# Second convolution by four phases of the position on 32-by-32 array tiles, one read-back of its input, other PSUM banks at the end

## The chip, the cores and the metric

The kernel runs on one core of a Trainium2 chip. The metric is the device time of one execution in microseconds; the median of three runs before the change is 1615.36 us (1615.16 to 1615.81). The program is written by hand for five engines (TensorE, VectorE, ScalarE, GpSimd, and SyncE, which issues every DMA); each engine has its own list of instructions and waits on semaphores.

## The reference, cut to what matters

`x` is 64 sequences of 32 tokens of 512 numbers. The last lines of the reference are a residual chain: a conditional mix of channels and a state-space block with group norm and output projection are added to `x`, then a grouped one-dimensional convolution with a context term, then a feed-forward layer with a cluster mask:

```
x = x + attn(cond(x, cond_128, ...), ...)
x = x + cond2(x, cond_128, weight, c_weight, bias=fside)   # what the change is about
x = x + ffn(x, weight, bias, centroids, assignments)
```

The convolution treats the 32 tokens of a sequence as channels and the 512 numbers as positions: 32 channels in, 32 out, 4 groups of 8 channels, 9 taps, padding 4:

```
out = lax.conv_general_dilated(x, weight, (1,), [(4, 4)], ('NCH','OIH','NCH'), feature_group_count=4)
out = out + einsum('nd,od->no', c, c_weight)[:, :, None] + bias[None, :, None]
```

The feed-forward layer computes `x @ weight.T + bias` (512 by 512), a softmax over 64 clusters, and zeroes rows and columns by whether any softmax value passes 0.01. The kernel's FFN takes the convolution's result as its input, and its output is added to the running `x`.

## The kernel before, in words

A token tile is four sequences, 128 tokens, on 128 partitions; there are 16 of them, T = 0 to 15, held for the whole run in `acc[128, 16, 520]` with four zero columns at either side of the 512. The main part is a loop over 32 stages (`stage(n)`, L556 on TensorE), each a pair of a half of the batch and one of 8 groups; a stage projects ten 128-row blocks (`proj`, L421) with fp32r high and low parts, and between them runs the scan's small matmuls (`Y`, L497, `G_all`, L484), the output projection of the stage before (`O`, L531) and its statistics (`S`, L516). `add_out` (L1084) adds the result to `acc`. The last stage is called END (n = 31). The diff changes nothing in the loop but access patterns.

After the last stage comes the part that the change is about. SyncE writes each finished tile to DRAM (`store_x2`, L307) and reads it back as `G_of(T)` with tokens as channels (`load_G`, L312): the input of the convolution for one tile is read four times, each time shifted by one position, so that partition 32j + channel holds the sequence shifted by j. `load_G` has four DMAs of 260 KB each per tile, into two tensors (`wh`, `wl`) that held projection weights.

TensorE then computes the convolution in pairs of tiles. `conv2(T)` (L589) covers taps 0 to 3 and 4 to 7: for each of four sequences one matmul of 128 rows by 32 columns over 512 positions, twice, into the PSUM bank `PP[T % 2]`. `conv2_last_tap(T)` (L600) covers tap 8 for both tiles of the pair with 32-by-32 matmuls, each (sequence, tile) on another row strip of the array. All these are plain fp32 matmuls; in the trace one fp32 matmul is two MATMUL instructions.

Per tile, ScalarE copies the convolution's bank to SBUF with the context bias (`x3_biased`, L854), TensorE transposes it (`turn`, L610, four 128-column transposes, alternately into banks 6 and 3), ScalarE and VectorE split it into high and low parts (`x3_high`, L862; `x3_low`, L1153), and TensorE multiplies by the feed-forward weights in two column halves of 288 (`ffn(T, 1)`, `ffn(T, 0)`, L622). VectorE's `ffn_rows(T)` (L1167) handles maximum, softmax sums, mask and bias; `dense` (L1157) reads the FFN's banks.

TensorE's program after stage 31 (L669 to L700) is: `conv2(0)`, `conv2(1)`, `conv2_last_tap(0)`, then the rest of END (`O(END, 0)`, `Y`, `O(END, 1)`, `S`, `turn(0)`, `O(END, 2)`, `O(END, 3)`, `S`), then steps 2 to 17. A step s is: on even steps below 16 the convolution of tiles s and s + 1, then `turn(s - 1)`, `ffn(s - 2, 1)`, and for tiles below LATE = 10 also `ffn(s - 2, 0)`. The halves `ffn(T, 0)` of tiles 10 to 15 come after the last step. Then the column maximum is transposed (L694), the mask of rows is spread by matmuls (L697, L698), `choose` (L1200, VectorE) writes the results of tiles 4 to 15 to `acc`, `finish_apart` (L1391, GpSimd) those of tiles 0 to 3, and SyncE stores them in the order `order_out`. For tiles 10 to 15 GpSimd runs `late_base` (L1380) beforehand.

At the start SyncE loads `x`: tiles 0 to 3 by four DMAs (L285), tiles 4 to 15 by three DMAs of 1 MB (L292), and then projection blocks one by one into a ring of three (`load_w`, L294). GpSimd makes the low part of each block (`split_w_lo`, L1315) and two thirds of the mixing weights (`mixing_weights`, L1304).

Of the kernel before, what the change touches and what calls it, by code (L numbers as in the profile page):

```python
# [22 lines left out]
P_CW, P_CB, P_D, P_NW, P_B0, P_B1, P_DTB, P_AL, P_FS, P_END = 0, 192, 240, 272, 304, 305, 306, 307, 308, 309  # L23
# [7 lines left out]
FB = ((SEG[0], PP[2]), PY)  # L31
# [47 lines left out]
def before(n, i, back=2):  # L79
    return divmod(4 * n + i - back, 4)  # L80

# [5 lines left out]
def adaln_attn_ffn_kernel(nc, x, emb, gin, b2, wbank, biask, w_in, w_dt, w_out, prm, cst, cw4, ctxw,  # L87
                          w_ffn, b_ffn, asg, x2s, out):
    ctx = ExitStack()
    with ctx:  # L90
# [48 lines left out]
        cxb = sb("cxb", [128, NT])  # L139
# [27 lines left out]
        cxt = yq[:, 128:192].rearrange("p (t b) -> p t b", b=4)  # L167
# [10 lines left out]
        asi, asf, ohf = xs[0:64, 2, :].bitcast(I32), xs[0:64, 3, :], Lt[0:64, 0:512]  # L178
# [3 lines left out]

        def G_of(T):
            w = (wh, wl)[(T % 4) // 2][:, :, :].rearrange("p a b -> p (a b)").bitcast(F32)
            return w[:, 2080 * (T % 2):2080 * (T % 2) + 2080].rearrange("p (b c) -> p b c", b=4)
# [8 lines left out]
        def ffn_bank(T, c):  # L194
            if c == 0 and T >= LATE + 2:
                return (PP[0], PP[1], FB[0][1], FB[1][1])[T - LATE - 2]
            return FB[T % 2][c]

# [3 lines left out]
        def O_bank(n, i):  # L202
            return PP[2] if (n, i) == (END, 1) else PO[i]
# [13 lines left out]
        ld_x = [None] + [signal(f"ld_x{c}", step=16) for c in range(1, 4)]  # L217
# [4 lines left out]
        ld_G = [signal(f"ld_G{r}", [(T, j) for T in range(r, NT, 4) for j in range(4)], 16) for r in range(4)]  # L222
# [39 lines left out]
        conv_ok, x3_ok, x3t = signal("cv", range(NT)), signal("x3", range(NT)), signal("xt", range(NT))  # L262
# [13 lines left out]
        def sync_program(e):  # L276
# [7 lines left out]
            for T in range(4):  # L284
                e.dma_start(acc[:, T, 4:516], x[T]).then_inc(ld_x0[T].sem, 16)  # L285
# [26 lines left out]
            def load_G(T):  # L312
                sp.wait_ge(x2_out[T // 4], 4 * (T // 4) + 3)
                if T < 4:
                    sp.wait_ge(proj_ok, (END, 4 if T % 2 == 0 else 8))
                else:
                    sp.wait_ge(conv_ok, T - 4)
# [24 lines left out]
            for T in (0, 2, 1, 3):  # L342
                load_G(T)
# [3 lines left out]
            sp.wait_ge(T_ok, (END, 3))  # L347
            for j in range(4):
                sp.wait_ge(xsd_ok, (END, j))
# [3 lines left out]
            for T in range(4, NT):  # L353
                if T == 9:
                    for t in range(12, 16):
                        store_x2(t)
                load_G(T)
# [4 lines left out]
        def tensor_program(e):  # L362
# [7 lines left out]
            def mix_tile(T, n):  # L370
# [19 lines left out]
                for k in range(4):  # L390
                    mm = e.matmul(PS[:, bank, 128 * k:128 * k + 128], acc[:, T, 4 + 128 * k:132 + 128 * k], bd,  # L391
# [124 lines left out]
            def S(n, group):  # L516
                pe.wait_ge(ys2, (n, group[-1]))
                if group[0] == 0:
                    if n:
                        pe.wait_ge(var_ok, (n - 1, 3))  # L520
                    else:
                        pe.wait_ge(cx_ok, 0)
                elif group == (1, 2):
# [3 lines left out]
                for i in group:  # L527
                    mm = e.matmul(PS[:, PG, 256 + i:257 + i], yss[:, i, :], C[:, C_ONE:C_ONE + 1], start=True, stop=True)  # L528
                mm.then_inc(S_ok.sem, 1)

            def O(n, i):  # L531
# [8 lines left out]
                elif i == 1:  # L540
                    pe.wait_ge(evac_ok, (n, 7))
                else:
                    pe.wait_ge(y_ok, (n, 3))
                q = 0
# [6 lines left out]
            def context():  # L551
                pe.wait_ge(ld_cx)
                pe.wait_ge(G_masked, 0)
                e.matmul(PS[:, PG, 128:192], yq[:, 0:128], eT, start=True, stop=True).then_inc(cx_pe.sem, 1)
# [34 lines left out]
            def conv2(T):  # L589
                pe.wait_ge(ld_G[T % 4], (T, 3))  # L590
                if T >= 2:
                    pe.wait_ge(x3_ok, T - 2)
                else:
                    pe.wait_ge(evac_ok, (END, 8 + T))
                for q, off in enumerate((0, 4)):
                    for b in range(4):
                        e.matmul(PS[32 * b:32 * b + 32, PP[T % 2], :], w4[:, q, :], G_of(T)[:, b, off:off + 512],  # L597
                                 start=(q == 0), stop=False)

            def conv2_last_tap(T):  # L600
                for b in range(4):
                    for t in (T, T + 1):
                        r = (b + t) % 4
                        p = slice(32 * r, 32 * r + 32)
                        mm = e.matmul(PS[32 * b:32 * b + 32, PP[t % 2], :], w4[p, 2, :], G_of(t)[p, b, 8 - r:520 - r],
                                      start=False, stop=True)
                        if b == 3:
# [901 lines left out]
```

## Time and profile before

| | before |
|---|---|
| median of 3 runs | 1615.36 us |
| profiled execution, its own time | 1614.37 us |
| its span, first to last instruction | 1612.4 us |
| TensorE busy | 1587.4 us, 98% |
| VectorE busy | 1049.8 us, 65% |
| ScalarE busy | 845.7 us, 52% |
| GpSimd busy | 787.5 us, 49% |
| mean granted TensorE clock | 0.997 |
| DMA, data moved | 93.19 MB |

Times in the trace are counted from the span's start. The profiled execution took 2.0 us more than its span. Matmul durations in the trace overlap each other, since matmuls are pipelined; the time that a row of the chain of waits gives to a run of matmuls does not overlap with the next row, so the prediction takes its costs there.

### The profile page before, as it was taken

The numbers are of one execution on the slowest core, as the hardware profiler recorded it, in microseconds if no ns is written. First come the engines' busy times: TensorE is split into PE (matmuls) and PEld (weight loads), VectorE is DVE, ScalarE is ACT, GpSimd is POOL, SyncE is SP. The second block draws the span as 40 slices with busy tenths as digits, with TensorE's granted clock in tenths as the row PEclk, the third lists the DMA queues.
The fourth block names the chain that finished last, engine by engine and source line by source line (L and its number), as shares of the span: only waits on it lengthen the run. The fifth ranks groups of instructions, "written<-read, shape, count | busy, mean of one in ns | idle before, by whom it ended". The sixth has DMA issues, their size and how long they took to land.

```text
span 1612.4 us, 32430 instructions
## 1 busy us (share of the span) xinstructions
PE 1587.4 (98%) x13001; PEld 1275.0 (79%) x13001; DVE 1049.8 (65%) x1707; ACT 845.7 (52%) x1372; POOL 787.5 (49%) x747
## 2 busy tenths in 40 slices
PE   8999999999999999999999999999999999999998
PEld 6778888888888888877777888888888888888666
DVE  6876666565656667576776656565766656565545
ACT  4654546555555555555455555555555655554321
POOL 3564645546363644544345454536454554633306
PEclk9999999999999999999999999999999999999999
DMA  5111102011111102011012111112020111113892
GB/s 191 59 54 33 41 21 66 28 53 40 40 53 34 51 12 64 27 53 40 22 50 77 53 40 40 54 34 59 10 64 21 53 40 47 47 36 85 200 210 107
DMA packets 50293, 93.19 MB, mean 58 GB/s; under 512 B 5664, under 2 KB 6304, under 8 KB 50144
## 3 DMA queue, kind: packets, MB, share of 16 engines
q1 hardware_dynamic: 50144, 91.11, 19.6%
q8 instruction: 104, 1.70, 0.5%
q14 instruction: 45, 0.37, 0.1%
HBM read 82.64 MB, written 8.45 MB: 56 GB/s over the span
## 4 chain that ended last, share of the span: by engine, by line
PE 86%; ACT 6%; DVE 3%; issue 3%; POOL 2%; POOLq 0%; DVEq 0%; ACTq 0%
PE PS L438 49%; PE PS L547 20%; PE PS L513 4%; PE PS L481 3%; PE PS L639 2%; ACT L798 2%; PE PS L597 2%; ACT big L791 1%; PE PS L528 1%; ACT Lt L798 1%; DVE cb L1023 1%; PE PS L391 1%; PE PS L493 1%; ACT oh L717 1%; PE PS L388 1%
## 5 line engine op out<-in xcount | busy, mean ns | idle before, releaser
L438 PE MATMUL PS<-xh,wh 128*128 128x512 f32 x1280 | 520.0, 406 | 0.6 <-DVE xl L955 0.6
L438 PE MATMUL PS<-xh,wl 128*128 128x512 f32 x1280 | 500.3, 391 | 0.0
L438 PE MATMUL PS<-xl,wh 128*128 128x512 f32 x1280 | 500.2, 391 | 0.0
L1023 DVE SCALAR_TENSOR_TENSOR cb<-PS,P,cb 128x496 f32<-128x496 f32 (+2 forms) x576 | 412.4, 716 | 130.6 <-ACT cb L759 117.0
L1318 POOL TENSOR_TENSOR wl<-rw,wh 128x512 fp32r<-128x512 f32 x160 | 212.6, 1334 | 187.4 <-ACT wh L710 172.3
L1338 POOL TENSOR_TENSOR ysum<-yq 128x256 f32<-128x256 f32 x128 | 109.4, 855 | 361.7 <-ACT yq L806 361.7
L438 PEld LDWEIGHTS PS<-xh,wl 128*128 128x128 f32 x1280 | 240.5, 188 | 53.1
L438 PEld LDWEIGHTS PS<-xh,wh 128*128 128x128 f32 x1280 | 240.8, 188 | 51.4 <-issue 1.0
L438 PEld LDWEIGHTS PS<-xl,wh 128*128 128x128 f32 x1280 | 241.2, 188 | 44.6
L759 ACT ACTIVATE cb<-PS,P 128x512 f32<-128x512 f32 x192 | 148.5, 774 | 205.1 <-PE PS L438 205.1
L1053 DVE TENSOR_TENSOR big<-Lt,gmt 128x512 f32<-128x512 f32 x128 | 102.3, 841 | 153.4 <-ACT Lt L798 153.4
L547 PE MATMUL PS<-oh,yh 128*128 128x512 f32 x512 | 200.0, 391 | 0.3 <-issue 0.3
L547 PE MATMUL PS<-oh,yl 128*128 128x512 f32 x512 | 199.2, 389 | 0.0
L547 PE MATMUL PS<-ol,yh 128*128 128x512 f32 x512 | 199.2, 389 | 0.0
L806 ACT ACTIVATE yq<-y 128x512 f32<-128x512 f32 x128 | 81.0, 633 | 209.0 <-DVE y L1067 196.7
L766 ACT ACTIVATE big<-PS 128x512 f32<-128x512 f32 x128 | 76.2, 595 | 148.6 <-PE PS L438 148.2
L781 ACT ACTIVATE big<-cb 128x512 f32<-128x512 f32 x192 | 119.5, 623 | 63.4 <-DVE cb L1023 63.4
L1092 DVE SCALAR_TENSOR_TENSOR acc<-PS,rs,acc 128x512 f32<-128x512 f32 x128 | 93.1, 749 | 84.5 <-issue 46.9
L1355 POOL TENSOR_TENSOR rs<-vr,mh 128x1 f32<-128x1 f32 (+1 forms) x95 | 57.0, 600 | 164.4 <-DVE vr L1082 164.3
L1043 DVE TENSOR_TENSOR dtx<-PS,dtt 128x512 f32<-128x512 f32 x128 | 82.0, 682 | 59.9 <-PE PS L481 59.6
L547 PEld LDWEIGHTS PS<-oh,yh 128*128 128x128 f32 x512 | 96.1, 188 | 21.0 <-issue 0.8
L547 PEld LDWEIGHTS PS<-oh,yl 128*128 128x128 f32 x512 | 96.1, 188 | 20.0
(204 smaller groups left out, 2177.6 us busy)
## 6 DMA issues: line engine op xcount, KB each, us to landing
rw<-in_w_in SPq DMA_DIRECT2D x160, 256.0 KB, 2.7
ro<-in_w_out SPq DMA_DIRECT2D x64, 256.0 KB, 2.8
x2s<-acc SPq DMA_DIRECT2D x16, 260.0 KB, 5.4
out_x<-acc SPq DMA_DIRECT2D x16, 256.0 KB, 2.6
acc<-in_x SPq DMA_DIRECT2D x3, 1024.0 KB, 9.4
wh<-x2s SPq DMA_DIRECT2D x8, 260.0 KB, 5.0
wl<-x2s SPq DMA_DIRECT2D x8, 260.0 KB, 5.7
wh<-x2s SPq DMA_DIRECT2D x8, 259.5 KB, 5.6
```

The lines of the kernel that those rows point to most:

```text
L438: mm = e.matmul(PS[:, proj_bank(n, m), :], w[:, m, 128 * k:128 * k + 128], v[:, k, a:a + 512], start=(i == 0), stop=(i == 11))
L547: mm = e.matmul(PS[:, O_bank(n, i), :], v[:, r, 128 * j:128 * j + 128], w[:, j, :], start=(q == 0), stop=(q == 11))
L759: e.activation(cb[:, z % 2, :], PS[:, proj_bank(n, m), :], ACT.Identity, bias=P[:, P_CB + c:P_CB + c + 1], scale=P[:, P_CW + 4 * c + 3:P_C ...
L766: e.activation(gate[:, m - 6, :], PS[:, proj_bank(n, m), :], ACT.Silu).then_inc(evac_ok.sem, 1)
L781: e.activation(dst, cb[:, (6 * n + m) % 2, :], ACT.Silu).then_inc(silu_ok.sem, 1)
L806: e.activation(yq[:, :], y[:, i % 2, :], ACT.Square).then_inc(yq_ok.sem, 1)
L1023: e.scalar_tensor_tensor(out=cv[:, :, d:32], in0=pv[:, :, 0:32 - d], scalar=P[:, P_CW + 4 * c + 3 - d:P_CW + 4 * c + 4 - d], in1=cv[:, :, ...
L1043: e.tensor_tensor(dtx[:, r, :].rearrange("p (j v c) -> p j v c", j=4, v=2), PS[:, b0:b0 + 2, 256 * r:256 * r + 256].rearrange("p v (j c) - ...
L1053: e.tensor_tensor(Mb[:, i % 2], bc(Lt[:, 256 * i:256 * i + 256].rearrange("p (h o t) -> p h o t", h=8, o=1), 128, 8, 2, 32), bc(gmt[:, i, ...
L1092: e.scalar_tensor_tensor(out=acc[:, T, 4:516], in0=PS[:, O_bank(n, i), :], scalar=rs[:, i:i + 1], in1=acc[:, T, 4:516], op0=ALU.mult, op1= ...
L1318: e.tensor_tensor(wl[:, m, :], rw[:, q % RW, :], f(wh[:, m, :]), ALU.subtract).then_inc(w_lo.sem, 1)
L1338: e.tensor_tensor(ysum[:, :], yq[:, 0:256], yq[:, 256:512], ALU.add).then_inc(ys1.sem, 1)
```

## The change

The 512 positions of a token are stored phase by phase: position 4j + f stands at column 128f + j. Inputs, projection weights, output weights and FFN weights are permuted on the host, and the output is permuted back. In `acc` each phase has one zero column on either side (4 times 130 = 520). So a partition of the read-back tensor can hold one (channel, phase) pair, and a group of 8 channels with 4 phases fills 32 partitions. A convolution output of phase f' is then a sum over three shifts a of the phase columns: 3 matmuls of 32 by 32 over 128 columns for each channel group, sequence and tile.

`conv2(c)` now does four tiles, 4c to 4c + 3, in one go, with 4 x 3 x 4 x 4 = 192 matmuls on all 16 array tiles. Output channel group g goes to PSUM bank g, so the four banks 0 to 3 hold four token tiles. The input is read back once per tile (one DMA in pieces of 520 bytes instead of four DMAs). The loads and the final stores of `acc` are in pieces of 512 bytes.

```diff
-            def conv2(T):
-                pe.wait_ge(ld_G[T % 4], (T, 3))
-                if T >= 2:
-                    pe.wait_ge(x3_ok, T - 2)
-                else:
-                    pe.wait_ge(evac_ok, (END, 8 + T))
-                for q, off in enumerate((0, 4)):
-                    for b in range(4):
-                        e.matmul(PS[32 * b:32 * b + 32, PP[T % 2], :], w4[:, q, :], G_of(T)[:, b, off:off + 512],
-                                 start=(q == 0), stop=False)
-            def conv2_last_tap(T):
...
+            def conv2(c):
+                if c:
+                    pe.wait_ge(x3_ok, (4 * c - 1, 3))
+                else:
+                    pe.wait_ge(evac_ok, (END, 9))
...
+                pe.wait_ge(ld_G[c], 4 * c + 3)
+                for t in range(4):
+                    for a in range(3):
+                        for k in range(4):
+                            for b in range(4):
+                                g = (b + k) % 4
+                                p = slice(32 * g, 32 * g + 32)
+                                mm = e.matmul(PS[32 * b:32 * b + 32, g, 128 * t:128 * t + 128], w4[p, a, :],
+                                              G_of(4 * c + t)[p, b, a:a + 128], start=(a == 0), stop=(a == 2))
+                mm.then_inc(conv_ok.sem, 1)
```

The read-back, the loads and the stores on SyncE:

```diff
-                for j in range(4):
-                    src = bass.AP(x2s.tensor, T * 128 * XP + j, [[XP, 32], [32 * XP, 4], [1, 520 - j]])
-                    e.dma_start(G_of(T)[32 * j:32 * j + 32, :, 0:520 - j], src).then_inc(ld_G[T % 4].sem, 16)
+                src = bass.AP(x2s.tensor, T * 128 * XP, [[XP // 4, 128], [32 * XP, 4], [1, XP // 4]])
+                e.dma_start(G_of(T), src).then_inc(ld_G[T // 4].sem, 16)
...
-                e.dma_start(acc[:, T, 4:516], x[T]).then_inc(ld_x0[T].sem, 16)
+                e.dma_start(tokens(T), phases(x[T])).then_inc(ld_x0[T].sem, 16)
...
-            e.dma_start(yq[:, 0:128], ctxw).then_inc(ld_cx.sem, 16)
+            e.dma_start(Lt[:, 512:1024], ctxw).then_inc(ld_cx.sem, 16)
             for c in range(1, 4):
-                e.dma_start(acc[:, 4 * c:4 * c + 4, 4:516], x[4 * c:4 * c + 4].rearrange("t p d -> p t d")).then_inc(ld_x[c].sem, 16)
+                for T in range(4 * c, 4 * c + 4):
+                    e.dma_start(tokens(T), phases(x[T])).then_inc(ld_x[c].sem, 16)
...
-                e.dma_start(out[T], acc[:, T, 4:516]).then_inc(stored.sem, 16)
+                e.dma_start(phases(out[T]), tokens(T)).then_inc(stored.sem, 16)
```

with `phases(a)` = `a.rearrange("p (f j) -> p f j", f=4)` and `tokens(T)` = the 4 x 128 inner columns of `acc[:, T]`.

The banks at the end: the convolution takes banks 0 to 3, so the statistics of END go to bank 4, and the output projections of END go to banks 7, 6, 5, 7. The fourth shares bank 7 with the first and waits for its sum. `turn` has only bank 6, and `ffn(T, 0)` only bank 7:

```diff
-FB = ((SEG[0], PP[2]), PY)
+FB = ((SEG[0], PY[0]), (SEG[0], PY[1]))
...
-            return PP[2] if (n, i) == (END, 1) else PO[i]
+            return (SEG[0], PT, PY[1], SEG[0])[i] if n == END else PO[i]
...
+                if (n, i) == (END, 3):
+                    pe.wait_ge(acc_ok, (n, 0))
...
             def turn(T):
-                pe.wait_ge(x3_ok, T)
-                if T >= 2:
-                    pe.wait_ge(x3_lo, T - 2)
...
+                pe.wait_ge(x3_ok, (T, 3))
+                if T:
+                    pe.wait_ge(x3_lo, T - 1)
+                else:
+                    pe.wait_ge(acc_ok, (END, 1))
...
+                elif c == 0 and T:
+                    pe.wait_ge(dense_ok, (T - 1, 0))
...
+                else:
+                    pe.wait_ge(acc_ok, (END, 3))
```

ScalarE copies a tile out of four banks by four instructions of 128 columns, one step of the loop at a time:

```diff
-                e.activation(xs[:, T % 2, :], PS[:, PP[T % 2], :], ACT.Identity, bias=cxb[:, T:T + 1]).then_inc(x3_ok.sem, 1)
+                for g in range(4):
+                    e.activation(xs[:, T % 4, 128 * g:128 * g + 128], PS[:, g, 128 * (T % 4):128 * (T % 4) + 128], ACT.Identity,
+                                 bias=cxb[:, g, T:T + 1]).then_inc(x3_ok.sem, 1)
```

The order of TensorE after stage 31 (on the other engines `x3_high(0)` moves behind the copies of the FFN weights, `x3_biased(2)` and `(3)` ahead of them, and `x3_low(0)` behind the last `add_out`):

```diff
             conv2(0)
-            conv2(1)
-            conv2_last_tap(0)
             O(END, 0)
             Y(END, 2)
             Y(END, 3)
             O(END, 1)
             S(END, (0, 1))
-            turn(0)
             O(END, 2)
             O(END, 3)
+            turn(0)
             S(END, (2, 3))
             for step in range(2, NT + 2):
-                if step < NT and step % 2 == 0:
-                    conv2(step)
-                    conv2(step + 1)
-                    conv2_last_tap(step)
+                if step + 2 < NT and step % 4 == 2:
+                    conv2((step + 2) // 4)
                 if step <= NT:
                     turn(step - 1)
```

The context term needs four small matmuls (one for each channel group) where it had one, and its weights are 256 KB instead of 64 KB. VectorE and GpSimd read and write `acc` as 4 x 128 columns instead of 512.

## Rows read from the trace of the kernel before

**Rows 1.** The page: engines' busy time, and the chain that ended last by engine.
```profile
PE 1587.4 (98%) x13001; PEld 1275.0 (79%) x13001; DVE 1049.8 (65%) x1707; ACT 845.7 (52%) x1372; POOL 787.5 (49%) x747
...
PE 86%; ACT 6%; DVE 3%; issue 3%; POOL 2%; POOLq 0%; DVEq 0%; ACTq 0%
```

**Rows 2.** Windows: stretch, length; PE, PEld, DVE, ACT, POOL busy; PEclk, DMA share, GB/s.
```profile
1520.00:1540.00 20.00, 20.00 (x179) 12.71 (x179) 7.47 (x26) 5.32 (x13) 0.00 (x0) 1.00 0.91 221
```

**Rows 3.** Chain of waits, 1490 us to the end: start us, us, what.
```profile
1490.33 3.59 PE PS L597 x32
1493.91 1.02 PE PS L605 x16
...
1502.99 5.72 PE PS L547 x24
...
1514.23 3.19 PE PS L639 x24
1517.42 0.44 PE PS L619 x4
...
1568.97 3.58 PE PS L597 x32
...
1593.19 0.20 PE PS L694
```

**Rows 4.** The same view, small fp32 matmuls of a stage of the loop.
```profile
1457.14 1.09 PE PS L513 x64
1458.23 0.39 PE PS L493 x32
```

**Rows 5.** Timeline of GpSimd and VectorE in the rest of END: start, us, engine, line.
```profile
1494.26 1.84 POOL L1347 TENSOR_TENSOR yl<-big,yh 128x512 fp32r<-128x512 f32 x1
...
1507.71 1.41 DVE L1092 SCALAR_TENSOR_TENSOR acc<-PS,rs,acc 128x512 f32<-128x512 f32 x2 [0.88 <-issue]
...
1512.64 1.41 DVE L1092 SCALAR_TENSOR_TENSOR acc<-PS,rs,acc 128x512 f32<-128x512 f32 x2 [0.86 <-issue]
```

**Rows 6.** Timeline of VectorE in a step with both FFN halves.
```profile
1521.08 0.76 DVE L1165 TENSOR_TENSOR big<-PS,pb 128x288 f32<-128x288 f32 x2 [0.92 <-PE PS L639]
...
1522.32 0.49 DVE L1195 TENSOR_SCALAR big<-big,qs 128x512 f32<-128x512 f32 x1
```

**Rows 7.** Timeline of VectorE and GpSimd in the late steps and at the end.
```profile
1586.78 0.68 DVE L1155 TENSOR_TENSOR yl<-PS,yh 128x512 fp32r<-128x512 f32 x1
1586.94 0.67 POOL L1383 TENSOR_TENSOR big<-pb,qs 128x288 f32<-128x288 f32 x1 [3.89 <-DVE qs L1188]
...
1589.01 0.68 DVE L1155 TENSOR_TENSOR yl<-PS,yh 128x512 fp32r<-128x512 f32 x1
1589.51 0.67 POOL L1383 TENSOR_TENSOR big<-pb,qs 128x288 f32<-128x288 f32 x1
...
1597.46 1.28 POOL L1396 TENSOR_TENSOR big<-big,y 128x512 f32<-128x512 f32 x1 [0.26 <-ACT y L921]
```

**Rows 8.** Groups by line and form, 1430 us to the end: busy us, mean ns, idle before.
```profile
L860 ACT ACTIVATE big<-PS,cxb 128x512 f32<-128x512 f32 x16 | 10.2, 687 | 34.1 <-PE PS L605 34.1
...
L875 ACT ACTIVATE PS<-PS,s 128x64 f32<-128x64 f32 x16 | 4.6, 288 | 21.3 <-DVE s L1177 21.3
```

**Rows 9.** Timelines of ScalarE and GpSimd at the start of the run.
```profile
22.44 0.62 ACT L710 CAST wh<-rw 128x512 fp32r<-128x512 f32 x1 [1.61 <-DMA rw<-in_w_in]
...
23.14 1.29 POOL L1318 TENSOR_TENSOR wl<-rw,wh 128x512 fp32r<-128x512 f32 x1 [2.18 <-ACT wh L710]
```

**Rows 10.** DMA queues in 2.4:2.8 and 13:20: packets, MB, share of 16 engines.
```profile
q1 hardware_dynamic: 136, 0.15, 108.7%
...
q1 hardware_dynamic: 1367, 2.73, 104.4%
```

**Rows 11.** DMA queue in 1597.5:1612.4, and the issues of the final stores.
```profile
q1 hardware_dynamic: 2304, 4.20, 74.3%
...
L324 SPq DMA_DIRECT2D out_x<-acc x16: 332/447/561, 1596.7 to 1608.4; - x16
```

More of the change, by code:

```diff
@@ L80, in before, with phases @@
     return divmod(4 * n + i - back, 4)
+def phases(a):
+    return a.rearrange("p (f j) -> p f j", f=4)
 def last_acc(T):
@@ L216, in adaln_attn_ffn_kernel @@
         ld_x0 = [signal(f"ld_x0{T}", step=16) for T in range(4)]
-        ld_x = [None] + [signal(f"ld_x{c}", step=16) for c in range(1, 4)]
+        ld_x = [None] + [signal(f"ld_x{c}", step=64) for c in range(1, 4)]
         ld_w = [signal(f"ld_w{r}", [divmod(q, 10) for q in range(r, 160, RW)], 16) for r in range(RW)]
@@ L341, in sync_program @@
             e.dma_start(raws[2], w_ffn[2]).then_inc(ld_f[2].sem, 16)
-            for T in (0, 2, 1, 3):
+            for T in range(8):
                 load_G(T)
@@ L346, in sync_program @@
             e.dma_start(bB, b_ffn).then_inc(ld_bf.sem, 16)
-            sp.wait_ge(T_ok, (END, 3))
-            for j in range(4):
-                sp.wait_ge(xsd_ok, (END, j))
+            sp.wait_ge(M_ok, (END, 3))
             e.dma_start(asi, asg).then_inc(ld_as.sem, 16)
@@ L352, in sync_program @@
                 store_x2(T)
[L353 to L356, printed above, removed]
+            for T in range(8, 12):
+                load_G(T)
+            for T in range(12, 16):
+                store_x2(T)
+            for T in range(12, 16):
                 load_G(T)
@@ L390, in mix_tile @@
                 for k in range(4):
-                    mm = e.matmul(PS[:, bank, 128 * k:128 * k + 128], acc[:, T, 4 + 128 * k:132 + 128 * k], bd,
+                    mm = e.matmul(PS[:, bank, 128 * k:128 * k + 128], tokens(T)[:, k], bd,
                                   start=False, stop=(k == 3))
@@ L522, in S @@
                         pe.wait_ge(cx_ok, 0)
+                    if n == END:
+                        pe.wait_ge(y_ok, (n, 3))
                 elif group == (1, 2):
@@ L1196, in ffn_rows @@
                 else:
-                    e.scalar_tensor_tensor(out=d, in0=d, scalar=qs[:, T:T + 1], in1=acc[:, T, 4:516],
+                    e.scalar_tensor_tensor(out=phases(d), in0=phases(d), scalar=qs[:, T:T + 1], in1=tokens(T),
                                            op0=ALU.mult, op1=ALU.add).then_inc(res_ok.sem, 1)
@@ L1218, in vector_program @@
             e.tensor_copy(yh[:, 0, :], Lt[:, 0:512]).then_inc(ones.sem, 1)
-            e.memset(acc[:, :, 0:4], 0.0).then_inc(pad.sem, 1)
-            e.memset(acc[:, :, 516:520], 0.0).then_inc(pad.sem, 1)
+            for c in (0, 129):
+                e.memset(acc[:, :, :].rearrange("p t (f c) -> p t f c", f=4)[:, :, :, c], 0.0).then_inc(pad.sem, 1)
             dve.wait_ge(ld_c)
@@ L1272, in vector_program @@
             y_out(END, 3)
-            x3_low(0)
             variance(END, (0, 1))
@@ L1282, in vector_program @@
             add_out(END, 3)
+            x3_low(0)
             dve.wait_ge(ld_as)
+            dve.wait_ge(yq_ok, (END, 3))
             e.tensor_copy(asf, asi).then_inc(hot_in.sem, 1)
```

136 lines of the change are left out of this document (68 added, 68 removed).

## The prediction, made before the changed kernel was run

> **What bounds the kernel now.** I read the page first: TensorE is busy 98% of the span and carries 86% of the chain that ended last [rows 1], so what counts is TensorE's time, wherever it is not waiting. Next the table of windows: in the stretch after the stages TensorE is still busy 20.00 of 20.00 us at clock 1.00, VectorE 7.47 and ScalarE 5.32, while the DMA engines are at a share of 0.91 [rows 2]. The full queue is no bound, since TensorE has no gap there; what the change takes from the DMA is worth nothing by itself. Then the chain of waits gives the lengths [rows 3]: a pair of tiles costs 3.59 + 1.02 = 4.61 us of convolution; the first FFN tile starts at 1514.23, step 12 at 1568.97, and the column maximum is transposed at 1593.19. So the tail splits into END (to 1514.23), steps 2 to 11 (54.7 us), steps 12 to 17 with one FFN half each (24.2 us), and the finish (19.2 us).
>
> **The price of the new convolution.** Before, 8 pairs x 4.61 = 36.9 us. After, 4 groups of 192 matmuls, each two instructions: 384 in a group, 24 on each of 16 array tiles. One array tile streams 512 columns in two instructions while eight of them finish in 1.02 us [rows 3], so an instruction of 512 columns takes at most 0.51 us, and 32 instructions of 512 columns on four tiles take 3.59, which is 0.449 each. A quarter of the columns is 0.112 us, so 24 x 0.112 = 2.7 us if all 16 tiles run side by side. Can the starts keep up? 32 instructions over 32 columns take 0.39 us, 12.2 ns each, on four tiles; 64 of 64 columns take 1.09 us, 17 ns each [rows 4]. Both run on four array tiles at a time, which may be what paces them, so 12.2 ns is an upper bound for the distance of two starts; 2.7 us for 384 would need 7 ns. The pair's last tap put 16 instructions of 0.449 us into 1.02 us on eight tiles, so eight run together. Sixteen at once, with four row strips writing four banks on the same PSUM partitions, no row shows. The bounds: 2.7 us (16 at once), 384 x 12.2 ns = 4.7 us (starts at the rate of [rows 4]), 48 rounds x 0.112 = 5.4 us (eight at once), 96 x 0.112 = 10.8 us (four at once). I take 2.9 us, near the first, because the last tap, with twice as many tiles as the other taps, took only 0.12 us more than two instructions of 0.449 in a row. Changing to small tiles and back costs a further 0.15 beside each convolution: steps 2 to 11 hold 3.19 + 9 x 3.63 + four pairs, which leaves 4.7 to 4.8 for a pair of 4.61.
>
> A rule speaks against this. The Trainium skill (TensorE: Matmul & The Clock Gate, "Wait — 56ns, not 53.3ns?") says that start-to-start of matmuls never falls below about 25 ns, however few columns; by it a group takes 384 x 25 ns = 9.6 us and the convolution 38 us, more than now. The trace disagrees for small tiles: 12.2 ns in [rows 4]. By the rule the run would end with the slower rival below.
>
> **Steps 2 to 11 (from the first FFN tile to step 12).** Before: 3.19 + 9 steps of 3.63 (0.44 + 3.19) + four pairs of 4.76 = 54.9, against 54.7 in [rows 3]. After: 3.19 + 32.7 + two groups of 3.05 (steps 6 and 10) = 42.0. Gain 12.7 us. Who might take over? VectorE: after the second half of an FFN tile it needs 1.7 to 1.9 us (1521.08 to 1522.8 [rows 6], some 0.2 more where the last operation also adds `acc`), then x3_low 0.68 [rows 7], and the next turn, which now waits for it because it has one bank, is 3.63 us behind; 1.0 us is left. Bank 7 alone for the second half: its reader is the first of [rows 6], 0.4 us, and the next writer comes 0.44 + 1.6 us later. ScalarE: four copies of 128 columns between 0.69 / 4 = 0.17 and 0.29 us each [rows 8]; I take 0.28, 1.1 us a tile, 2 us of work in a step of 3.6. If that cover went, a step would be as long as the longest of these chains, some 4.6 us. The reads of the input are a quarter of the bytes, and are issued as early as before; nothing waits for them.
>
> **Steps 12 to 17.** Two of the eight pairs stood here with six turns and halves; now no convolution stands here. TensorE would need 0.44 + 1.6 = 2.0 us a step, but VectorE's chain (x3_low, maximum, exponent on ScalarE, bias, reciprocal, mask) repeats every 2.23 us (1586.78 to 1589.01 [rows 7]). So VectorE takes over: 1.95 us left over from tile 9, x3_low 0.65, four periods of 2.25, and rows of the last two tiles 1.6 + 1.5, and 0.4 of turnarounds: 15.1 us. Gain 24.2 - 15.1 = 9.1 us.
>
> **END.** Only 1.2 us is lost here, and the shorter convolution does not help. O(END, 0) waits for its y_low, which ends as the one of the next tile starts, at 1494.26 [rows 5], so a convolution that ends at 1493.2 instead of 1494.93 gives back 0.5 us at most. Then the new wait: O(END, 3) shares bank 7 with O(END, 0) and waits for add_out(END, 0). That one waits for rstd, which stands on GpSimd behind the splits and sums of tiles 2 and 3; add_out(END, 0) came at 1507.71 [rows 5]. With the 0.5 us its first half ends near 1508.0. TensorE did O(END, 2) and (END, 3) in 5.72 us from 1502.99 [rows 3], the second of them from 1505.85; now it stands about 2.5 us before it. Queued behind it: turn(0), S(END, (2, 3)), the second convolution. S ends near 1511.6; variance, rstd and the last two add_out (1.41 us [rows 5]) end about 2.5 us later, then come x3_low(0), now behind them, and turn(1): the first FFN tile at about 1515.4 instead of 1514.23. Bounds: -1.5 (the wait costs nothing and the convolution's gain stays) and +3.
>
> **The start.** x comes in pieces of 512 bytes instead of 2 KB. From [rows 10]: 2 KB packets take 104.4% x 16 x 7 us / 1332 = 88 ns, 1.25 KB packets 108.7% x 16 x 0.4 / 120 = 58 ns (without those of 4 bytes), so a 512 B piece is about 28 ns, and 2 KB in four pieces 112. For 8 rows an engine and 16 tiles that is 16 x 8 x 0.024 = 3.1 us more of a queue that is full in both windows, and 0.19 MB more of context weights 0.5 us (2.73 MB took 7). The fourth projection block, issued at 17, stands behind it; ScalarE waited for it (1.61 us), then GpSimd, which was free 2.18 us earlier [rows 9], then the mixing weights on the same engine. That chain decides when TensorE goes on. So the start pays +3.5 us; bounds 0 (other slack) and 4.5. Twelve issues instead of three on SyncE are about 7 us and end at 16, just before the next one. The three extra context matmuls: 0.5 us on TensorE.
>
> **The finish.** Stores too are in 512 B pieces. Now 74.3% x 16 x 14.9 us / 2048 = 86.5 ns a packet, 0.69 us a tile [rows 11]; with 112 ns 0.90. GpSimd frees four stores every 2.6 us (two operations of 1.3 for each of its tiles, the first of them at 1597.46 [rows 7]), which need 2.8 us now and 3.6 then. After two early stores, 14 x 0.90 from 1601 (the first of GpSimd's, and 1 us from issue to data) end at 1613.6. Now the last issue at 1608.4 [rows 11] bounds it: 0.5 of issue, 1 and two tiles of 0.69 still under way make 1611.3. So +2.0 us with the rounding down. Late_base on GpSimd has a period of 2.57 (1586.94 to 1589.51 [rows 7]) against 2.25 of VectorE, six times: it ends 0.3 us later than the mask: +0.3. Bounds 0 and +6, since no row shows a write in such pieces.
>
> **Sum.** 1612.4 + 4.0 + 1.2 - 12.7 - 9.1 + 2.3 = 1598.1 us of span; with the 2.0 us around it 1600.1, and the median lay 1.0 above the profiled execution: 1601 us, 0.9% faster.
>
> **Rivals.**
> (a) Eight tiles at a time: the banks or the starts pace a group to 5.4 us. For it: no row has four row strips writing the same partitions. Against: eight lose nothing. Four groups x 2.5 less the cover in END (1 us) = +9: 1610 us.
> (b) Small pieces cost more than 28 ns, in HBM writes above all: +4 to +6 at the end and one more at the start: 1607 us. For it: only reads gave the price.
> (c) The single banks pace the steps: turn waits for x3_low, x3_low stands behind the rows of the tile before, and each of the 9 steps is 4.6 us: +9, 1610 us. Against: 1.0 us is left in the account above.
> (d) The slower side: only four array tiles stream at a time, because matmuls start in order and the next on a busy tile holds up the rest. A group costs 10.8 us: four times 7.9 more is 31.6, of which about 1 hides in END: 1631 us. From about 7 us a group on the gain is gone (14.5 / 4 + 2.9, END's cover counted). Against: eight together in the last tap. (The Trainium skill's floor, quoted above, would put a group at 9.6 us and the run at 1627 us; of the 0.07 below it has 0.02.)
>
> **How the numbers follow.** The forecast 0.66 with its own range 1595 to 1606; (a) 0.11, (b) 0.09, (c) 0.05, (d) 0.07, and 0.02 that gains and losses cancel. Of (a) 0.02 and of (c) 0.01 end within 0.2%. The range of 1594 to 1611 takes in (a) to (c) and leaves out (d) and the far ends. A measurement tells 0.2%, 3.2 us, from no change: faster 0.66 + 0.09 + 0.09 + 0.04 = 0.88, same 0.05, slower 0.07.
>
> **What would show it.** Right: a convolution group at 2.7 to 3.2 us in the chain of waits; a gap of TensorE of 2 to 3 us before the fourth output projection of END; steps of 3.6 us; late steps with VectorE in the chain at 2.2 us a tile; ScalarE's wait for the fourth block 3 to 4 us longer; the last stores at a DMA share near 1. Wrong: a group above 4.7 us; TensorE waiting for x3_low in steps 3 to 11; a start that does not move; stores above 30 ns a piece.

## The result, and the profile after

The changed kernel takes 1624.98 us (median of 4 runs, 1622.7 to 1627.6) against 1615.26 (4 runs, 1614.98 to 1615.81) for the kernel before: ratio 1.0067, 95% interval 1.0054 to 1.008 (the two medians alone stand at 1.0060). It is 0.6 to 0.7% slower where 0.9% faster was forecast. Its profiled execution took 1626.38 us, with a span of 1624.4.

First the page of the changed kernel, with the engines' busy time, the share of the chain that ended last, and the queue that brings the instructions.

```profile
PE 1577.4 (97%) x14159; PEld 1287.6 (79%) x14159; DVE 1051.0 (65%) x1707; ACT 852.7 (52%) x1420; POOL 785.3 (48%) x747
...
q8 instruction: 113, 1.85, 0.5%
...
PE 84%; ACT 6%; issue 4%; DVE 3%; POOL 2%; POOLq 0%; DVEq 0%; ACTq 0%
```

TensorE works 10 us less than before [rows 1] and the kernel is 12 us longer: the chain has gained "issue", time in which TensorE waits for nothing that the profile shows. The next table cuts the rest of the run at the same places in both kernels: from the first convolution to its end, END to the second convolution, that convolution to the first FFN tile, steps 2 to 11, steps 12 to 17, finish. Columns as in [rows 2]. The changed kernel:

```profile
1494.69:1504.61 9.92, 6.55 (x385) 5.21 (x385) 6.53 (x8) 2.40 (x4) 6.05 (x6) 0.90 0.21 71
1504.61:1524.30 19.69, 16.36 (x136) 12.98 (x144) 7.08 (x9) 9.22 (x25) 9.30 (x9) 0.88 0.37 109
1524.30:1533.24 8.94, 6.35 (x390) 5.38 (x391) 3.04 (x7) 0.28 (x1) 0.70 (x1) 1.00 0.18 65
1533.24:1587.18 53.94, 47.51 (x1047) 45.12 (x1046) 25.64 (x84) 21.64 (x71) 0.00 (x0) 1.00 0.09 23
1587.18:1602.76 15.58, 14.37 (x105) 13.19 (x103) 11.56 (x47) 7.23 (x25) 10.57 (x15) 1.00 0.00 0
1602.76:1624.40 21.64, 10.27 (x65) 8.61 (x64) 11.98 (x21) 0.59 (x1) 13.29 (x12) 0.87 0.66 195
```

And the kernel before:

```profile
1490.33:1494.93 4.60, 4.60 (x49) 1.00 (x49) 4.47 (x8) 1.97 (x4) 2.38 (x2) 1.00 1.09 220
1494.93:1509.05 14.12, 13.86 (x129) 11.34 (x132) 6.49 (x11) 6.96 (x12) 11.44 (x14) 1.00 1.06 271
1509.05:1514.23 5.18, 5.18 (x55) 1.70 (x55) 4.32 (x7) 0.49 (x1) 2.07 (x2) 1.00 0.22 45
1514.23:1568.97 54.74, 54.74 (x473) 40.01 (x475) 26.24 (x87) 16.57 (x41) 0.00 (x0) 1.00 0.90 202
1568.97:1593.19 24.22, 23.85 (x202) 15.74 (x201) 11.55 (x47) 7.38 (x21) 10.90 (x14) 1.00 0.16 31
1593.19:1612.40 19.21, 11.80 (x65) 10.14 (x64) 12.55 (x21) 0.59 (x1) 13.94 (x13) 0.87 0.58 220
```

Against the sum of the prediction: the start (to the first convolution) +4.36 (forecast 4.0); END +14.65 (1.2): the three stretches last 9.92 + 19.69 + 8.94 = 38.55 us instead of 23.90; steps 2 to 11 -0.80 (-12.7): 53.94 against 54.74; steps 12 to 17 -8.64 (-9.1): 15.58 against 24.22; the finish +2.43 (2.3): 21.64 against 19.21. They add up to the 12.0 us between the spans. Three terms are right within half a microsecond (what stands behind them is taken up at the end). Both that fail contain the convolution, and there the chain of waits of the changed kernel shows what [rows 3] had no trace of:

```profile
1494.69 2.23 PE PS L617 x117
1496.91 1.25 issue
1498.16 1.91 PE PS L617 x101
1500.07 2.11 issue
1502.18 2.42 PE PS L617 x104
...
1547.30 2.25 PE PS L617 x125
1549.55 1.25 issue
1550.80 1.89 PE PS L617 x95
1552.69 1.85 issue
1554.54 1.48 PE PS L617 x74
...
1556.60 3.19 PE PS L650 x24
1559.79 0.44 PE PS L629 x4
```

A group is not 2.9 us but 8.7 in the loop (1547.30 to 1556.02) and 9.9 for the first one: three bursts of matmuls, and between them two gaps in which TensorE stands still although nothing that the profile knows of holds it up. The other two groups take 8.35 us (from 1524.30) and 9.13 (from 1570.64). The FFN steps around them have the forecast's 0.44 + 3.19.

What a gap waits for stands in the DMA view of the same group, 1547.3 to 1556.1, in 40 slices of 0.22 us (busy tenths of the 16 DMA engines), and below it the only queue that moved anything:

```profile
DMA  0000020000000000000003000000000000000020
...
q8 instruction: 3, 0.05, 2.3%
```

Three packets of about 16 KB (0.05 MB) in the queue "instruction", which begin in slices 6, 22 and 39: at 1548.4, 1551.9 and 1555.7. A packet is under way for 1.1 us (2.3% x 16 x 8.8 us / 3), and the bursts behind the gaps begin 2.4 and 2.6 us after the start of the first and second packet. TensorE has 384 MATMUL records and as many weight loads in a group (x385 in the first window), 768 instructions. The chain of waits does not count every record of a burst; the timeline of TensorE does, and it gives this group's bursts 161, 128 and 95 records. The middle one:

```profile
1550.80 1.89 PE L617 MATMUL PS<-wh,w 32*32 32x128 f32 x128 [1.25 <-issue]
```

128 matmul records with their 128 weight loads are 256 instructions, and the count of packets below makes that exactly one packet. The middle burst has 128 records in all four groups, while the first one has 148, 147, 161 and 174, and the third the rest. The whole run fits as well: the page of the kernel before has 104 packets in that queue, this one 113. The old convolution had 8 x 96 = 768 instructions in all, the new one has 4 x 768 = 3072; 2304 more in 9 more blocks is 256 instructions a block.

### The profile page after: what moved, and what is told of

It reads as the page before. It is cut to its first block, busy times and chain, and to the rows that moved or that the text cites. A ratio compares the mean times of both kernels' runs of the same rounds, so it can differ in the third digit from the quotient of the medians.

```text
span 1624.4 us, 34751 instructions
## 1 busy us (share of the span) xinstructions
PE 1577.4 (97%) x14159; PEld 1287.6 (79%) x14159; DVE 1051.0 (65%) x1707; ACT 852.7 (52%) x1420; POOL 785.3 (48%) x747
## 4 chain that ended last, share of the span: by engine, by line
PE 84%; ACT 6%; issue 4%; DVE 3%; POOL 2%; POOLq 0%; DVEq 0%; ACTq 0%
PE PS L447 48%; PE PS L558 20%; PE PS L522 4%; PE PS L490 3%; PE PS L650 2%; ACT L805 2%; PE PS L617 1%; ACT big L798 1%; ACT Lt L805 1%; PE PS L539 1%; DVE cb L1035 1%; PE PS L400 1%; PE PS L502 1%; PE PS L377 1%; PE PS L397 1%
```

## The experiments

Two theories. **Supply**: the instructions come in blocks of 256; TensorE works a block of these small matmuls off in 1.9 us (the middle burst; the first bursts of some 2.2 us hold more than a block) and gets the next one only every 3.5 to 4 us. **Array**: 16 tiles in four row strips, written to four banks on the same partitions, do not stream together (the prediction's rivals (a) and (d)), and the gaps only sort the time differently. On the three chips of the experiments the kernel before took 1613.5 to 1613.9 us (medians), 1.3 to 1.8 us less than in the section above; no run of the changed kernel stands beside it there. So totals are compared with that kernel before, and the argument rests on the lengths of groups inside each run.

### One matmul over four tiles: 48 a group

```
-                for t in range(4):
-                    for a in range(3): ...   # out: 128 columns of one token tile
+                G = w[:, 0:4 * XP].rearrange("p (t b c) -> p t b c", t=4, b=4)
+                    for a in range(3): ...
+                            mm = e.matmul(PS[32*b:32*b+32, g, :].rearrange("p (t j) -> p t j", t=4),
+                                          w4[p, a, :], G[p, :, b, a:a + 128], ...)
```

> The same convolution with the four token tiles in one matmul of 512 columns (4 x 128 in the access pattern): 48 matmuls a group instead of 192, the same columns, array tiles and banks. Theory S (supply of instructions): a group is slow because its 768 instructions (384 weight loads, 384 matmul instructions) are three blocks of 256, and a new block comes only every 3 to 3.5 us, while TensorE works one off in 2.2 us. Then 192 instructions a group are less than a block: 2.7 to 3.2 us a group instead of 8.4 to 9.9, no gap inside, and END loses its low clock too: median 1600 to 1604 us. Theory B (banks or array): four row strips that write four banks on the same partitions cannot stream together, so 5.4 us (eight at a time) or 9 to 10.8 us (four at a time) whatever the number of instructions: 1611 us or more.

Measured: 1603.38 us (4 runs, 1602.41 to 1604.96), ratio to before 0.9934 (0.9918 to 0.9951). The same columns, array tiles, row strips and banks, a quarter of the instructions. Its chain:

```profile
1535.98 3.35 PE PS L618 x91
```

A group takes 3.35 us without a gap (a little above the 2.7 to 3.2 expected, and 0.45 above the prediction's 2.9), and the queue of the instructions is back at 104 packets. The array theory falls: eight tiles at a time would have needed 5.4 us, so sixteen tiles do run side by side. This is also the kernel that the forecast of 1601 us, 0.9% faster, describes (0.66% measured): steps 2 to 11 from 1521.95 to 1564.69, 42.7 us, where 42.0 was forecast.

### Two tiles in a matmul: 96 a group

```
-                for t in range(4):
+                for t in (0, 2):      # each matmul over 256 columns of two token tiles
```

> Two token tiles in one matmul of 256 columns: 96 matmuls, 384 instructions a group. Theory S: one and a half blocks, so one or at most two gaps: 4 to 6 us a group. Theory B: as with 128 columns, 8.4 to 9.9 us; the 512-column form would not differ either.

Measured: 1605.78 us (one run); groups of 4.84, 3.96, 4.02 and 3.96 us, and one gap of 0.21 us, in the first. So 384 instructions of 256 columns take little more than 192 of 512. I had expected a gap or two in each group: where these 384 instructions last 3.96 us, the next block comes in time; the gaps appear between this form and the next.

### All 192 matmuls, fewer columns

```
+                                cols = 128 if a == 0 else 32
-                                ... 128 * t:128 * t + 128 ...  a:a + 128
+                                ... 128 * t:128 * t + cols ... a:a + cols
```

> The same 192 matmuls and 768 instructions a group as the changed kernel, but the second and third shift cover 32 of their 128 columns (the rest of their part of the convolution is left out): half of the streamed columns. Theory S: a group stays at 8 to 9.9 us, with the gaps where they were. Theory B: it falls with the columns, to 4 to 5.5 us.

Measured: 1629.88 us (one run); groups of 8.94, 8.54, 9.34 and 9.06 us. The third in the chain:

```profile
1547.48 1.79 PE PS L618 x99
1549.27 2.28 issue
1551.55 1.84 PE PS L618 x71
1553.40 1.90 issue
1555.30 1.52 PE PS L618 x53
```

Half of the columns are gone and the group has not become shorter. Its bursts are somewhat shorter (1.79 instead of 2.25 us for the first) and the gap behind the first is longer (2.28 instead of 1.25 us); from second burst to third it is 3.75 us here (1551.55 to 1555.30) and 3.74 in the changed kernel (1550.80 to 1554.54). Time goes by blocks, not by columns. (The run as a whole is 5 us longer than the changed kernel's although its groups are not: the FFN tiles behind the second, third and fourth group, at a granted clock of 1.00 there, had 0.91 (1531.5 to 1547.4), 0.95 (1556.8 to 1572.2) and 0.75 (1581.3 to 1590) here.)

### The group cut in two around the FFN half

```
-                    conv2((step + 2) // 4)
+                    conv2((step + 2) // 4, range(0, 2))
                 ...  turn and the first FFN half ...
+                    conv2((step + 2) // 4, range(2, 4))
```

> The changed kernel with a group of the loop cut in two: two tiles, then the transpose and 12 FFN matmuls (some 2 us of TensorE), then the other two tiles. Same instructions, columns and banks. Theory S: fetching goes on under the transpose and the FFN half, so the convolution's own time in a group of the loop falls by 1.5 to 3 us from 8.4 to 9.1. Theory B: no change beyond 0.3 us.

Measured: 1620.23 us (one run). The last group:

```profile
1566.33 2.52 PE PS L617 x135
1568.85 1.45 issue
1570.29 0.46 PE PS L617 x18
...
1571.34 1.60 PE PS L651 x12
1572.94 2.70 PE PS L617 x152
```

The convolution's own time is 2.52 + 1.45 + 0.46 + 2.70 = 7.13 us instead of 9.13. The 1.6 us of large FFN matmuls cover the arrival of one block, and the second gap is gone. In the third group the convolution's own time is 7.36 us instead of 8.72 (a little less gained than the 1.5 us expected at least). In the second it is 6.49 instead of 8.35, but there a gap has moved into the FFN tile, whose matmuls were not changed (timeline of TensorE):

```profile
1531.77 0.40 PE L651 MATMUL PS<-xh 128*128 128x288 f32 x1 [1.25 <-issue]
```

Between the gap before it (the burst from 1524.16) and this one stand 256 records, 45 and 192 of the convolution, 4 of the transpose and 15 of the FFN: with their loads 512 instructions, exactly two blocks. A gap comes where a block ends, whatever matmul stands there. The same matmuls in another order, so it is not their cost but their density.

### The same 192 matmuls with half the instructions

```
-   w4[p, a, :], G_of(...)[p, b, a:a + 128]
+   w4[p, a, :].bitcast(bfloat16)[:, 1::2], G_of(...)[p, b, a:a + 128].bitcast(bfloat16)[:, 1::2]
```

> The changed kernel with the operands of the 192 small matmuls of a group read as 16-bit floats (the upper halves of the same numbers, so the convolution's values are rounded to that format and the output is not exact). Each matmul is then one load and one matmul instruction instead of two of each: 384 instructions a group instead of 768, with the same 192 matmuls, tiles, banks and 128 columns. Supply theory (16 KB blocks of 256 instructions, one every 3.3 to 3.5 us): one and a half blocks a group, one gap at most, 3 to 4.8 us a group instead of 8.3 to 9.9; total 1604 to 1611. Rival, a fixed cost of some 45 ns for each small matmul whatever it is made of: groups stay at 8.3 to 9.9 us, total 1622 to 1627.

Measured: 1603.69 us (one run). The first group in the chain of waits, then the second in the timeline of TensorE:

```profile
1494.13 1.44 PE PS L617 x144
1495.57 2.31 issue
1497.88 0.63 PE PS L617 x41
```

```profile
1517.20 1.80 PE L617 MATMUL PS<-wl,w 32*32 32x128 bf16 x192
```

One record a matmul now, 384 instructions a group, one and a half blocks: the groups come alternately with one gap (4.38 and 4.29 us) and with none (1.80 and 1.74). The page has 107 packets of instructions, half-way as it must be: 4 x 384 - 768 = 768 more instructions than before, three blocks. A fixed price of a small matmul would have kept 8 us. The gap is longer than in the changed kernel because the block is used up faster; from start to start it is 3.75 us again (1494.13 to 1497.88) and, in the third group, 3.85. The total is just below what was expected, since two groups had no gap at all and took 1.8 us, where 3 had been the least.

### The 512 B pieces alone

```
-                e.dma_start(tokens(T), phases(x[T]))          # and phases(out[T]) at the end
+                e.dma_start(acc[:, T, 4:516], x[T])           # and out[T]: whole rows of 2 KB
```

(The zero columns are set as in the kernel before.)

> The changed kernel with its x loads and final stores in whole 2 KB rows again instead of 512 B pieces (the tokens land at other places of the buffer, so the values computed are not those of the reference; all matmuls, sizes and orders are those of the changed kernel). It prices the small pieces by themselves. Supply theory and the sum of the prediction: the start comes back by about 3.5 us (the split of the second weight chunk starts near 23.3 instead of 26.84), the finish by about 2 us (from the last VectorE step to the end about 19.5 instead of 21.6), the convolution groups stay at 8.3 to 10 us; total 1618 to 1621. A rival that makes the small pieces a cause of the long groups (transfers of the instruction blocks queue behind them) would give groups that are shorter by a microsecond or more, total below 1616.

Measured: 1619.27 us (one run; the changed kernel took 1624.98, where the kernel before took 1615.26 and not 1613.47). The changed kernel's start, timeline of ScalarE and of GpSimd:

```profile
26.15 0.62 ACT L717 CAST wh<-rw 128x512 fp32r<-128x512 f32 x1 [4.37 <-DMA rw<-in_w_in]
```

```profile
26.84 1.30 POOL L1331 TENSOR_TENSOR wl<-rw,wh 128x512 fp32r<-128x512 f32 x1 [4.93 <-ACT wh L717]
```

and GpSimd with 2 KB pieces:

```profile
23.21 1.29 POOL L1332 TENSOR_TENSOR wl<-rw,wh 128x512 fp32r<-128x512 f32 x1 [1.60 <-ACT wh L718]
```

The split of the fourth block comes 3.63 us earlier, as forecast, and the first convolution 3.35 (1491.34). What the pieces do there stands in the timeline of SyncE, which issues the twelve loads of x and then the fourth block, first in the changed kernel, then with whole rows:

```profile
9.74 10.93 SPq L303 DMA_DIRECT2D acc<-in_x  x12
8.92 5.90 SPq L304 DMA_DIRECT2D acc<-in_x  x12
```

With pieces SyncE is busy issuing until 20.67 and issues the fourth block at 20.79; with whole rows it is done at 14.82 and issues the block at 18.21, as GpSimd's first split, which frees the buffer, ends (18.18; 18.48 in the changed kernel). From issue to ScalarE's cast it is then 5.36 us with pieces (26.15) and 4.30 without (22.51). So of the 3.6 us 2.3 are the time for which the free buffer waits for SyncE, 0.3 the later buffer, and 1.1 the transfer.

The finish is 18.5 us long (the transposes of the maximum at 1598.71, end at 1617.2) instead of 21.64: the pieces cost 3.1 us there, not 2. The difference is hidden in the forecast's net 2.3, because GpSimd's last additions became shorter (1.20 instead of 1.29 us, and VectorE's selection 0.71 instead of 1.01), which had been counted at nothing. The first, third and fourth groups take 9.51, 8.78 and 9.13 us: the pieces are no cause of the gaps.

### Moving one reciprocal root in END

The merged form, with GpSimd's rstd of the first two tiles between the splits and the sums of the last two, so that bank 7 comes free earlier.

```
             for i in (2, 3):
                 y_low(END, i)
+            rstd(END, (0, 1))
             for i in (2, 3):
                 y_sum(END, i)
-            rstd(END, (0, 1))
```

> The merged form (one matmul over four tiles, 48 a group) with one edit more: at stage 31's end GpSimd computes the reciprocal root of the first two tiles between splitting y of the third and fourth tile and forming the group sum, instead of after it. That frees PSUM bank 7 for O of the fourth tile earlier. In the merged form alone that O waited about 2.5 us and its last 12 matmuls then ran at the lower clock (4.46 instead of about 2.7 us). If the wait is real and ends with that bank: O(END,3) starts 2 to 2.8 us earlier and the total falls by 2 to 4.5 us, to 1599 to 1601.5. If GpSimd's later steps (the group sum of tile 3 and its reciprocal root, which the first FFN tile waits for) are pushed back by as much as the moved step takes (about 0.9 us), the gain is lost there: 1602.5 to 1604.5.

Measured: 1603.41 us (4 runs, 1602.54 to 1603.86), ratio to before 0.9933 (0.9917 to 0.995): nothing gained on 1603.38. First the changed kernel's wait for the bank (timeline of TensorE), then the lines of this one:

```profile
1518.94 0.47 PE L558 MATMUL PS<-oh,yh 128*128 128x512 f32 x1 [2.53 <-DVE acc L1104]
```

```profile
1509.32 0.39 PE L558 MATMUL PS<-oh,yh 128*128 128x512 f32 x1
...
1519.30 0.67 PE L630 MATMUL PS<-C,big 128*128 128x128 f32 x4 [2.96 <-DVE xl L1168]
```

The bank's wait is gone, and behind the second convolution there is one of 2.96 us for x3_low(0). VectorE comes to it late: it splits FFN weights until 1516.3 and only then computes the variance that GpSimd's second root and both additions need. The counted price (0.9 us of GpSimd) was not what ate the gain. From the first convolution to the first FFN tile it is 25.6 us instead of 26.9; the 1.3 us are lost again in the FFN tile behind the idle time, which takes 4.69 us instead of 3.18 (granted clock 0.65 in this stretch).

### The later x loads behind weight blocks

The same, with tiles 4 to 15 of x issued between the weight loads of stage 0.

```
-            for c in range(1, 4): ...          # x of tiles 4 to 15, in front of the fourth block
             for m in range(RW, 10):
                 load_w(0, m)
+                if m in (4, 6, 7):
+                    load_x((4, 6, 7).index(m) + 1)
```

> As the previous kernel, and the three later x loads (tiles 4 to 15, in 512 B pieces) are issued between the weight blocks of stage 0 instead of in front of the fourth of them. The start of the changed kernel waits 3.5 us longer for the weights that stand behind these pieces. If that is the whole of the start's loss, GpSimd's wait goes and the start gives 3.5 to 4 us back: total 1595 to 1598. If the same bytes merely delay a later weight block by as much (DMA is at 99 to 109% in the first 20 us and beyond), the loss only moves: 1599 to 1602. The groups stay at 3.35 us in either case.

Measured: 1596.52 us (4 runs, 1595.6 to 1599.26), ratio to before 0.9894 (0.988 to 0.9909), the fastest version of the study. GpSimd's wait for the fourth block:

```profile
21.38 1.28 POOL L1334 TENSOR_TENSOR wl<-rw,wh 128x512 fp32r<-128x512 f32 x1 [0.45 <-ACT wh L720]
```

0.45 us instead of 4.93; the first convolution starts at 1488.08, 6.3 us ahead of the kernel of the section above. The rest of the gain over that kernel is the first FFN tile, at full clock here (3.18 us). The order of loads was not tried in the merged form without the moved root.

### The same load order in the kernel before

> The kernel before, with the three later x loads (whole 2 KB rows) issued between the weight blocks of stage 0 instead of in front of the fourth of them. It says how much of the best version's gain belongs to the order of loads and how much to the convolution. In the kernel before GpSimd waited 2.18 us for the weights behind these loads, and the best version's start lies 2.2 us in front of that of the kernel before: the start should give 1.8 to 2.4 us here too, and nothing else changes: 1611 to 1612.5 against 1613.5. If the x loads merely push later weights back by as much: no change.

Measured: 1611.84 us (10 runs, 1610.16 to 1612.55) against 1613.54, ratio 0.9986 (0.9976 to 0.9995): 1.7 us between the medians, 2.3 by the ratio; the total is inside the expected 1611 to 1612.5. In the profiled execution, which lies at the low end of the runs, the split of the fourth block starts at 20.34 instead of 23.14. So some 2 of the best version's 17 us are to be had without a new convolution. The same order was worth 6.9 us in the section above (1603.41 to 1596.52), where x comes in small pieces.

## Why the prediction was wrong

**The step that failed** is the price of the new convolution: "2.7 us if all 16 tiles run side by side", taken as 2.9, with "384 x 12.2 ns = 4.7 us" as the bound by starts. Measured 9.92, 8.35, 8.72 and 9.13 us. Of the 8.72, 5.62 are bursts and 3.10 gaps. Both parts hang on the number of instructions, which the prediction put at 384 because it left out the weight loads.

- The array was judged right. Merged into 48 matmuls, the sixteen tiles deliver the same columns in 3.35 us; rivals (a) and (d) are refuted as mechanisms, though the time came out close to (d)'s.
- The pace of starts was read from rows that don't carry it. [rows 4] show 32 and 64 records; a burst there ends before a block does. Here 384 records in 5.62 us of bursts are 14.6 ns each (12.8 from start to start, without the running out of each burst), above the 12.2 ns that I called an upper bound, and twice the 7 ns that the 2.7 us needed.
- The supply of instructions was in no term. The queue "instruction" stands on the page of the kernel before with 104 packets and 0.5% of the DMA's time, and I passed over it as small. What had to be compared was the need: 768 instructions in 2.9 us is a block each microsecond; over the whole run of before it is one block in 15.5 us (1612.4 / 104).

The Trainium skill (Runtime: NRT & Kernel Launch, "Instruction fetch mechanics") gives the same block, 16 KiB or 256 instructions, fetched while the one before is executed, and says that crossing a boundary is "mostly hidden". The count of packets agrees with the size, and their starts, 1.06 to 1.80 us into a burst, with the order; the gaps of 0.46 to 2.37 us disagree with "hidden" for a queue of small matmuls.

The rule of the Trainium skill that the prediction weighed (TensorE: Matmul & The Clock Gate, "Wait — 56ns, not 53.3ns?"), about 25 ns from start to start, would have given 9.6 us a group and 1627 us, 2 us above the result. The runs do not bear out its mechanism: a record takes 14.6 ns in the bursts, and 9.1 ns in the one-pass form (1.74 us for 192). The closeness is chance: 8.72 us over 384 records, gaps included, is 22.7 ns.

**Steps 2 to 11**: two groups at 8.72 and 9.13 us, with 0.15 each for the turn behind them, instead of 3.05 are 12.05 us, against 11.9 missing. The cover that the prediction counted on (VectorE 1.0 us ahead, ScalarE's four copies) held: every other step is 3.63 us. In the merged form it held at 3.35 us a group as well, so rival (c) did not occur.

**END**: the new wait for bank 7 came as forecast, 2.53 us before O(END, 3). The two groups there cost 12.5 us more than 5.8. About 2.6 us more are the clock: after the waits and gaps 12 matmuls of O took 3.64 us in the first tile and 4.58 in the last against some 2.9 and 2.72; the granted clock was 0.80 and 0.63 in these two, 0.88 in the whole stretch. The prediction priced waits in END as if the work behind them kept its pace. Together that is 15.1 us where 13.45 are missing; which waits of END covered the other 1.6 I have not followed.

**Start**: the amount is right (4.36 for 4.0), the pieces in front of the fourth block are its cause, but the way is for the greater part another. The prediction counted 3.1 us of a fuller queue and let SyncE's twelve issues take about 7 us and end at 16, at no cost. They took 10.93 us and ended at 20.67; of the 3.6 us that the pieces cost, 2.3 are this issuing and 1.1 the transfer (the experiment with whole rows). That the sum fits is in part luck. Whether an issue of small pieces is long by itself or because the queue is full, no run separates: 0.63 us each for the first tiles, 0.83 for most of the later ones, 0.43 to 0.45 for whole rows.

**Steps 12 to 17, finish**: right, by the mechanism named in each (VectorE in the chain, 4.8 us for two tiles where 4.5 were counted; stores in pieces). For the finish two errors cancelled: pieces 3.1 instead of 2.0 us, and 0.7 given back by shorter operations of GpSimd and VectorE. A 512 B store piece costs 27 ns (83.9% x 16 x 14.9 us / 7392 packets), 108 ns for 2 KB, where the loads' rows had promised 112:

```profile
q1 hardware_dynamic: 7392, 3.67, 83.9%
```

**Rival (b)** did not occur: a piece is not dearer in a store.

**What a block's 3.7 us consist of** can be read from the start and duration that the trace has for every packet. In front of the eight bursts of the changed kernel that follow a gap, the packet takes 0.88 to 1.38 us, and the burst begins 1.34 to 1.49 us after the packet's end. The packet after that begins 1.06 to 1.15 us after the burst does in six of the eight, and 1.75 and 1.80 us in the other two. From the third group's second burst to its third that is 1.14, 1.21 and 1.39 us, 3.74 in all. So in these stretches a block's packet starts only when the block before it is being worked off, and the packet itself is about a third of the period.

Left open: what happens in the 1.1 us before a packet and in the 1.4 us behind it. That the lower clock follows the idle time was seen in each such place, but not in each run (the best version's first FFN tile had full clock after the same 2.96 us); what decides it was not tried.

## What to carry to other kernels

Count instructions, weight loads included, not only columns and tiles: where a stretch of TensorE needs 256 of them in less than about 3.7 us, and more than 250 to 380 in a row, it is the supply that sets the time, and the trace shows bursts with "issue" between them and packets in the queue "instruction". Make small matmuls wide (several token tiles in one access pattern) before spreading them over array tiles, or put large matmuls between them. And a small share of a queue on the page says nothing of a stretch that lives on it alone.

## What the runs showed of the hardware

- Sixteen 32 x 32 array tiles work together with four row strips writing four PSUM banks on the same partitions: 96 records of 512 columns in 3.35 us, where four tiles needed 3.59 us for 32 [rows 3].
- TensorE gets a block of 256 instructions every 3.5 to 4.0 us (14 to 16 ns an instruction) in a stretch that wants them faster; small fp32 matmuls use a block up in 1.9 us (128 records and their loads), one-pass ones in some 1.2 (an estimate, two thirds of the 1.80 us for 192 records). Of a period of 3.74 us, 1.1 pass before the packet starts, 1.2 are the packet, and 1.4 pass before TensorE goes on.
- In END the same 12 matmuls took 2.72 us at the clock of 2.4 GHz and, after 2.53 us of idle time, 4.58. The first four starts behind the idle time were still 0.23 to 0.31 us apart; from the fourth on (0.8 us later) they were 0.40 to 0.43 apart, the level of 1.2 GHz.
- Issuing a load of 256 KB took SyncE 0.44 us in whole rows of 2 KB (median of twelve, 0.43 to 0.57), and 0.83 in pieces of 512 B (0.55 to 1.49).
